# Flamingo-style decoder on one Trainium2 core: the first attention's context values centred by a matmul, its group loop in new orders

## The reference

```python
x = x + tanh(g_xattn[0]) * _L0_xattn_ref(_layernorm(x), ctx, ctx, ...)   # then seven more blocks
# inside, with q = layernorm(x), k = v = ctx, per head:
fg_matrix = cs[:, :, :, None] - cs[:, :, None, :]      # cs: running sum of log sigmoid(forget gate)
log_D = where(causal, fg_matrix, -inf) + igate         # i and f gates: [q, k, v] @ kernel + bias
max_log_D = max(log_D, axis=-1);  D = exp(log_D - max_log_D)
C = (q @ k.T / sqrt(dh)) * D
normalizer = maximum(abs(sum(C, axis=-1)), exp(-max_log_D))
h = (C / (normalizer + 1e-6)) @ v
mean = mean(h);  var = var(h)                          # over the 32 features of a head
out = (h - mean) * rsqrt(var + 1e-6) * outnorm_scale
```

## Time and profile before

| What | Value |
|---|---|
| median of 3 runs | 2186.36 us (2183.57 to 2186.93) |
| the profiled execution, its own time | 2186.99 us |
| its span | 2185.2 us, 41654 instructions |
| busy over the span | PE 88%, VectorE 73%, ScalarE 37%, GpSimd 30% |
| first attention | from 0 to about 149 us |
| in 42.1 to 149.0 us | PE 58.6, VectorE 74.3, ScalarE 50.3, GpSimd 58.5 us busy |

### The profile page before, as it was taken

How to read it: one execution, slowest core, us unless ns; L and a number is a source line. 1 busy time by engine, 2 the same in 40 slices (tenths; PEclk the granted TensorE clock), 3 DMA queues, 4 the chain that set the end, 5 groups by cost and what they waited for, 6 DMA issues and landing times. The chain is left out here.

```text
span 2185.2 us, 41654 instructions
## 1 busy us (share of the span) xinstructions
PE 1930.7 (88%) x14275; PEld 1025.3 (47%) x14275; DVE 1592.2 (73%) x3255; ACT 811.0 (37%) x1491; POOL 662.1 (30%) x903
## 2 busy tenths in 40 slices
PE   4659998998998978999999998979997999979965
PEld 2644444444444434555555554435663444436631
DVE  4768868878878866777777775757884666658978
ACT  4632112012012105555565553315652222226645
POOL 4551102102102104555555553445730000022301
PEclk8559999999999989999999999989997999999966
DMA  4402222222222231000000000000002533311001
GB/s 112 147 18 60 54 45 59 52 45 59 52 45 59 54 83 65 2 2 1 0 0 0 0 2 1 1 6 16 15 6 63 138 79 105 85 38 19 15 1 39
DMA packets 60079, 89.66 MB, mean 41 GB/s; under 512 B 23720, under 2 KB 42024, under 8 KB 55472
## 3 DMA queue, kind: packets, MB, share of 16 engines
q1 hardware_dynamic: 59952, 88.04, 16.4%
HBM read 80.85 MB, written 2.97 MB: 38 GB/s over the span
## 5 line engine op out<-in xcount | busy, mean ns | idle before, releaser
L1021 PE MATMUL l0f_acc<-l0f_z,w_all 128*128 128x512 f32 x512 | 228.8, 609 | 15.0 <-DVE l0f_z L1229 15.0
L916 POOL TENSOR_TENSOR l0f_v<-l0f_val,l0f_top 64x256 f32<-64x256 f32 x128 | 78.2, 611 | 488.1 <-DVE l0f_val L1191 479.5
L970 PE MATMUL l0f_work<-w_all,l0f_xs 128*128 128x512 f32 x384 | 183.5, 600 | 15.2 <-DVE l0f_val L1186 14.5
L1021 PEld LDWEIGHTS l0f_acc<-l0f_z,w_all 128*128 128x128 f32 x512 | 99.1, 195 | 144.1 <-issue 124.2
L241 POOL TENSOR_SCALAR var_eps<-mean_var 128x4 f32<-128x4 f32 (+1 forms) x64 | 14.6, 227 | 474.3 <-DVE mean_var L225 472.2
L1415 PE MATMUL l1x_proj_v<-l1x_wvo,l1x_cs 128*64 128x512 f32 x512 | 134.9, 605 | 0.1
L1191 DVE COPY_PREDICATED l0f_val<-l0f_oh,l0f_work 128x512 f32<-128x512 int32 x160 | 116.6, 729 | 23.7 <-PE l0f_work L970 7.5
L2826 DVE TENSOR_TENSOR l2f_hu<-l2f_act_g,l2f_pu 128x512 f32<-128x512 f32 x104 | 71.1, 684 | 68.8 <-ACT l2f_act_g L2752 67.4
L2752 ACT ACTIVATE l2f_act_g<-l2f_pg 128x512 f32<-128x512 f32 x104 | 61.5, 594 | 149.8 <-PE l2f_pu L2693 138.0
L2701 PE MATMUL l2f_acc<-l2f_hid,w_all 128*128 128x512 f32 x208 | 107.6, 599 | 10.3 <-DVE l2f_hid L2832 10.3
L1641 DVE TENSOR_TENSOR l1x_nm_q<-l1x_proj_q,l1x_rs_q 128x512 f32<-128x512 f32 x64 | 44.2, 691 | 90.3 <-POOL l1x_rs_q L1351 90.3
(11 more groups left out here) (389 smaller groups left out, 4413.1 us busy)
## 6 DMA issues: line engine op xcount, KB each, us to landing
l0f_first_mask<-onehots SPq DMA_DIRECT2D x32, 512.0 KB, 5.7
w_all<-onehots SPq DMA_DIRECT2D x32, 512.0 KB, 11.8
w_all<-combination SPq DMA_DIRECT2D x40, 256.0 KB, 5.3
w_all<-in_weights SPq DMA_DIRECT2D x1, 4640.0 KB, 16.7
l0x_m_b<-running_max SPq DMA_DIRECT2D x16, 256.0 KB, 4.6
w_all<-combination SPq DMA_DIRECT2D x16, 224.0 KB, 4.5
w_all<-combination SPq DMA_DIRECT2D x16, 192.0 KB, 4.2
w_all<-combination SPq DMA_DIRECT2D x16, 160.0 KB, 4.3
```

Of the source, the lines that this page charges most:

```text
L916: nc.gpsimd.tensor_tensor(v2[a * SEQ:(a + 1) * SEQ, t % 2, b, :, :], val[r, t % 2, :, :].rearrange("p (c a) k -> p c a k", a=2)[:, :, a, : ...
L970: nc.tensor.matmul(value_banks[e % 3][:, :], xs[:, t * P:(t + 1) * P], ve[:, e, :], start=True, stop=True).then_inc(ve_done, 1)
L1021: nc.tensor.matmul(acc[:, :], oe[:, n % E, n // E, :], z[:, n % Z, :], start=(n == 0), stop=(n == C * E - 1)).then_inc(acc_done, 1)
```

## The change

GpSimd's context means and its per-group subtraction go. TensorE centres instead: per group, four fp32 matmuls multiply the transposed context by a constant 128 x 128 matrix (identity minus 1/32 within each head), into the PSUM bank `turn`, and ScalarE copies the result into va (`copy_values`). va, hs and den get two buffers. The loops of VectorE and GpSimd are written in another order. The matrix adds 128 columns to the constants.

```diff
-        half_sum = [sb(f"half_sum{i}", [P, TILES // PARTS * NH, DH >> (i + 1)]) for i in range(4)]
-        ctx_mean = sb("ctx_mean", [P, TILES * NH])
...
-        va = sb("va", [P, N, E])
-        hs = sb("hs", [P, N, E])
-        den = sb("den", [P, 3, N])
+        va = sb("va", [P, 2, N, E])
+        hs = sb("hs", [P, 2, N, E])
+        den = sb("den", [P, 2, 3, N])
...
-                def context_means(i):
-                    pool.wait_ge(core.ctx_loaded[i], 16)
-                    w = TILES // PARTS
-                    src = core.ctx_tok[:, i * w:(i + 1) * w, :].rearrange("p j (h e) -> p (j h) e", h=NH)
-                    n = DH
-                    for k in range(5):
-                        n //= 2
-                        dst = half_sum[k][:, :, :] if k < 4 else \
-                            ctx_mean[:, i * w * NH:(i + 1) * w * NH].unsqueeze(2)
-                        nc.gpsimd.tensor_tensor(dst, src[:, :, 0:n], src[:, :, n:2 * n], ALU.add).then_inc(summed, 1)
-                        pool.wait_ge(summed, count(5 * i + k + 1))
-                        src = dst
...
-                    context_means(i)
-                nc.gpsimd.tensor_scalar(ctx_mean[:, :], ctx_mean[:, :], 1.0 / DH, None, ALU.mult).then_inc(mean_ready, 1)
...
-                pool.wait_ge(mean_ready, count(1))
-                pool.wait_ge(ones_set, count(2))
-
-                def centre_values(g):
-                    after(pool, pv_done, g)
-                    means = ctx_mean[:, g * N:(g + 1) * N].rearrange("p (t h) -> p h t", h=NH)
-                    nc.gpsimd.tensor_tensor(va[:, :, 0:DH].rearrange("p (h t) e -> p h t e", h=NH),
-                                            core.ctx_tok[:, g * G:(g + 1) * G, :].rearrange("p t (h e) -> p h t e", h=NH),
-                                            bcast(means, 3, DH), ALU.subtract).then_inc(va_ready, 1)
-
                 def inverse_deviation(g):
                     pool.wait_ge(var_ready, count(g + 1))
+                    after(pool, rs_ready, g)
...
                 for i in range(GROUPS + 5):
-                    if 0 <= i - 4 < GROUPS:
-                        apply_gate(i - 4)
+                    if 0 <= i - 5 < GROUPS:
+                        norm_gpsimd(core, nc, pool, ns, i - 5)
+                    if 0 <= i - 2 < GROUPS:
+                        inverse_deviation(i - 2)
                     if 0 <= i - 3 < GROUPS:
-                        inverse_deviation(i - 3)
-                    if 0 <= i - 1 < GROUPS:
-                        centre_values(i - 1)
-                    if 0 <= i - 4 < GROUPS:
-                        norm_gpsimd(core, nc, pool, ns, i - 4)
+                        apply_gate(i - 3)
...
+                def centre_values(g):
+                    after(pe, va_ready, g)
+                    pe.wait_ge(read, count(4 if g > 2 else 2))
+                    for t in range(G):
+                        ins = nc.tensor.matmul(turn[:, t * P:(t + 1) * P], core.ctxT[:, (g * G + t) * P:(g * G + t + 1) * P],
+                                               core.const("centre"), start=True, stop=True)
+                    ins.then_inc(centred, 1)
...
+                        pe.wait_ge(ones_set, count(2))
...
-                            ins = nc.tensor.matmul(po[r, at:at + E], cmat[r, n, :], va[r, n, :], start=True, stop=True)
+                            ins = nc.tensor.matmul(po[r, at:at + E], cmat[r, n, :], va[r, g % 2, n, :], start=True, stop=True)
...
                 for i in range(GROUPS + 5):
                     if 0 <= i - 1 < GROUPS:
+                        centre_values(i - 1)
                         scores(i - 1)
                     if i == 3:
+                        pe.wait_ge(va_ready, count(3))
                         turn_gates(1)
...
+                def copy_values(g):
+                    act.wait_ge(centred, count(g + 1))
+                    act.wait_ge(ones_set, count(2))
+                    after(act, pv_done, g - 1)
+                    nc.scalar.activation(va[:, g % 2, :, 0:DH].rearrange("p (h t) e -> p t h e", h=NH),
+                                         turn[:, :].rearrange("p (t h e) -> p t h e", t=G, h=NH), ACT.Copy)\
+                        .then_inc(va_ready, 1)
+
                 def copy_sums(g):
                     act.wait_ge(pv_done, count(g + 1))
-                    after(act, scaled_ready, g)
-                    nc.scalar.activation(hs[:, :, :].rearrange("p (i n) e -> p i (n e)", i=2),
+                    after(act, scaled_ready, g - 1)
+                    nc.scalar.activation(hs[:, g % 2, :, :].rearrange("p (i n) e -> p i (n e)", i=2),
                                          po[:, :].rearrange("p (i n) -> p i n", i=2)[:, :, 0:8 * E], ACT.Copy)\
                         .then_inc(hs_ready, 1)
...
                 for i in range(GROUPS + 6):
+                    if 0 <= i - 1 < GROUPS:
+                        copy_values(i - 1)
                     if 0 <= i - 2 < GROUPS:
                         copy_sums(i - 2)
...
-                    after(dve, factor_ready, g)
-                    nc.vector.reciprocal(den[:, 2, :], den[:, 1, :]).then_inc(inv_done, 1)
+                    after(dve, factor_ready, g - 1)
+                    nc.vector.reciprocal(den[:, g % 2, 2, :], den[:, g % 2, 1, :]).then_inc(inv_done, 1)
...
                 for i in range(GROUPS + 6):
-                    if 0 <= i - 3 < GROUPS:
-                        variances(i - 3)
-                    if 0 <= i - 5 < GROUPS:
-                        norm_apply(core, nc, dve, ns, i - 5)
-                    if 0 <= i - 4 < GROUPS:
-                        add_to_x(i - 4)
                     if i == 2:
                         running_max(1)
                         ch.done()
                     if i < GROUPS:
                         exponents(i)
+                    if 0 <= i - 2 < GROUPS:
+                        denominators(i - 2)
+                        square_sums(i - 2)
+                        variances(i - 2)
                     if 0 <= i - 3 < GROUPS:
                         scale(i - 3)
                     if 0 <= i - 1 < GROUPS:
                         decayed_scores(i - 1)
-                    if 0 <= i - 2 < GROUPS:
-                        denominators(i - 2)
-                        square_sums(i - 2)
+                    if 0 <= i - 5 < GROUPS:
+                        norm_apply(core, nc, dve, ns, i - 5)
+                    if 0 <= i - 4 < GROUPS:
+                        add_to_x(i - 4)
...
+    put("centre", np.eye(P) - (p[:, None] // 32 == p[None, :] // 32) / 32.0)
...
```

21 lines of the change are left out of this document (10 added, 11 removed).

## The result

| | before | changed |
|---|---|---|
| median of six runs each | 2186.64 us (2183.57 to 2188.03) | 2196.38 us (2192.86 to 2202.17) |
| the profiled execution, its own time | 2186.99 us | 2202.17 us |
| end of the first attention in it | 148.78 us | 161.76 us |
| from there to the end of the span | 2036.4 us | 2038.6 us |

The account below looks back on a forecast made before the run. The first attention was taken as a ring of waits with no engine full, VectorE's list setting the period. Loop +15.0, first denominators +1.6, tail +2.5 and opening -4.1 summed to +15.0 us on 2186.99: 2202 us, range 2187 to 2212.

Parts of the forecast that it names:

- the ring: Group loop: one turn becomes strictly serial, 10.5 us between products 1 to 4 and 12.8 for 4 to 7; +15.0 us.
- the two copies: Group loop: two ScalarE copies of some 512 columns, one after the other, 0.65 us each, 1.3 per turn.
- The 1.6 for the denominators: Group loop: denominators and variance, plus some 0.1 us to the next instruction, take 1.6 us of each turn.
- the late turns: Group loop from the fifth turn: xn behind the product and four transposes ahead of the values make turns 12.8 us.
- The first denominators: Before product 1: the first seven instructions on den and var now stand ahead of it; +1.6 us.
- Centring: TensorE in the group loop: four new matmuls per group, between 1.94 and 3.88 us, taken as 1.94.
- The fourth rival: Group loop: centring takes 3.88 us, adding 1.94 in six turns, +11.6 us, 2213.6 us; chance 0.06.
- The opening: Before the group loop: GpSimd's halving additions go, gaining between 1.9 and 6.4 us; the middle taken, -4.1 us.
- The tail: After product 7: four normalisations remain instead of three; bounds 0 and +4.8 us, middle taken, +2.5 us.
- The clock's rise (first): Group loop: TensorE's longer bursts raise its clock, its links halve and exponentials decide; +3.4 us, 2190.4 us; chance 0.15.
- The third: Group loop: VectorE's list stays the bound, relieved of GpSimd, period 8.8 us; faster kernel, 2180.9 us; chance 0.06.
- The second: From the opening on: the clock stays up, the feed-forward block starts warm; -2.2 us, 2184.8 us; chance 0.05.

Follow-up runs that it names:

- e7: Changed kernel with ScalarE copying and squaring the sums of group i-2 before copying the centred values of group i-1; 2196.72 us in one profiled execution.
- e2: Changed kernel with denominators, square sums and variances put behind the product on VectorE instead of ahead of it; 2200.42 us in one profiled execution.
- e1: Changed kernel with VectorE's normalisation xn first in the turn again, not behind the product; median 2193.78 us, ratio 1.0030 against before.
- e5: Changed kernel with the four centring matmuls of each group issued twice, writing the same result; 2206.93 us in one profiled execution.
- e9: Changed kernel with GpSimd's halving additions (context means) put back into the opening, result unused; 2208.44 us in one profiled execution.
- e6: e4's kernel with all eight groups centred in the opening and eight buffers for va; median 2172.57 us, ratio 0.9941 against before.
- e4: Changed kernel with VectorE's and GpSimd's loops back in their old orders, GpSimd without its subtraction; median 2182.35 us, ratio 0.9974 against before.

## Why the prediction was right, point by point

**The direction and the ring: right, to 0.2 us a turn.** 10.5 and 12.8 were forecast, 10.54 and 12.65 measured, and products 1 to 7 lie 69.6 us apart for a forecast of 69.9. The parts agree too: the two handovers of TensorE are 1.27 and 3.56 in both, scaling 0.63 for 0.61. Two parts were off and nearly cancelled: centring with its handover is 2.11 instead of 1.94 + 0.05, and the two copies 1.13 instead of 1.3, since the second starts 0.50 after the first (81.02, 81.52), less than its duration of 0.60. The 1.6 for the denominators holds too (1.64), but it rests on a choice of row that the prediction doesn't speak of. It read group 0, where nothing ran beside them; in five of the eight groups of before the first instruction took 1.13 beside GpSimd's gate multiplication, as here one turn ahead of the earlier trace rows:

```profile
86.34 1.13 DVE L739 SCALAR_TENSOR_TENSOR l0x_den<-l0x_hs 128x16 f32<-128x16 f32 x1
```

In the changed kernel it takes 0.18 to 0.19 in all eight groups, as GpSimd waits for the variances then. With 1.13 the sum would have been 11.5. That the ring is what was said is shown by e7 and e2, each of which opens it at one link and brings the early turns to 9.5, and e1 shows the late turns' 2.1 us to be xn's place.

**The first denominators: right.** +1.45 for +1.6. The interval is 11.9 to 12.6 us in the six kernels with the denominators ahead of the product and 10.4 to 10.9 in the four with them behind it, so the sign is sure and the size is not.

**Centring: a mis-sized term, by little.** Eight records of the four matmuls took 2.07 us, with 128 columns, for the lower bound of 1.94 that I took from 64. The weight loads are 1.78 in both cases (for the 64 columns in the earlier trace rows), so the reason for choosing the lower end holds. The fourth rival (3.88) is out. e5 shows that what is added to the centring is added to the turn (1.71 us in the turn from product 1, 1.28 in that from product 4).

**The opening: mis-sized.** -4.1 was the middle of -1.9 and -6.4; -6.2 came. The step that failed is taking the middle: |f| came 5.1 us earlier (32.72 for 37.84), so most of VectorE's delay was passed on, and another 1.0 was gained between |f| and product 0, where the prediction had the chain "shift as it is". e9 ties 5.8 to 6.3 us to the means, so their worth is near the upper bound (6.4). The changed kernel's profile gave back about 1 of it, most likely to the dip of the clock in its opening, and won the 1.3 in the second memory trip. That it came to nearly the upper bound in sum is these two cancelling. TensorE is now busy 5.00 of 5.00 us from 20 to 30, so a further gain in VectorE's normalisation would probably be worth little; no run tries it.

**The tail: about right.** +3.05 for +2.5, within 0 and 4.8.

**The sum.** +14.64 + 1.45 + 3.05 - 6.16 = +13.0 for +15.0; the 2 us between are the opening. The forecast of 2202 is met by the profiled execution's 2202.17 partly by chance: 2.2 of its +15.2 are from the unchanged rest. The median, 2196.4, is 5.6 lower: 2.0 of it the terms explain. The other 3.6 lie between this execution, the slowest of the six, and its fellows, of which there is no trace; whether their attention also ends 13.0 us later is not shown. One sum in the prediction is off: with opening and tail at their bounds its terms give +10.2 and +19.5, which is 2197.2 to 2206.5, not 2196 to 2209.

**The rivals.** The clock's rise (first) did not happen in the changed kernel but does in e5, so its weight was not idle. The third, VectorE's list as the bound, came true only in e6, once both TensorE's chain and the ring were out of the way; its turns, 7.5 to 8.8, are not the 8.8 for all six that the prediction took, as it had the late period of 9.7 stand for the shorter early ones too. The second is out: 0.50 from the first turn on. In e6 the third's effect was measured a second time, 1.11 us for 0.18; the Trainium skill's GPSIMD Engine Reference (Specifications) names contention in SBUF with VectorE instructions that have two inputs there, as this one has, and the trace agrees.

The Trainium skill's TensorE: Matmul & The Clock Gate (What's actually happening) has the low clock as the default, from which activity releases it. In the changed kernel it stayed at 0.50 through every turn, and in e5 it rose with the same pattern and four more 128 x 128 matmuls; the rule holds in direction, and no run here says what it asks for.

## What to carry to other kernels

- Where engines hand work round in a ring, write down the chain from one product to the next with its handovers before judging an order: a step that stands ahead of the shared operation joins the ring, and one behind it lies beside it. A sum from rows was right to 0.2 us a turn, while busy shares said nothing.
- A change made of several edits can hold a gain and a greater loss: undo the orders alone. Here, in the profiles, they cost 20 us on top of a gain of 7.
- Work that needs only loaded inputs is best put into a stretch where its engine waits anyway; ask then which engine's list is full.

## What the runs showed of the hardware

- The clock rose within a burst of TensorE when the 128 x 128 matmuls in it were doubled (0.63 and 0.71 in the two windows above), but not in bursts of small matmuls that kept the engine busy 5.00 of 5.00 us, nor with single centring. In e5 it fell back in the wait behind the burst. Nor was it a matter of busy time alone: in e4 TensorE was busy 4.66 to 5.00 us of every 5 from 85 to 120 us, and the clock stayed at 0.50. What separates these cases I cannot say from these runs.
- A small VectorE instruction that met a 512-column GpSimd operation took 0.33 to 1.20 us instead of 0.16 to 0.18, whichever of the small instructions it was. In each case that was looked at it ended 0.02 to 0.05 us behind GpSimd's operation: the factor of the earlier trace rows at 103.93 (GpSimd at 103.90), the denominators in e6 at 87.55 (87.51), the shortest one, in before, at 77.88 (77.83). So the price was what was left of GpSimd's operation, and it depends on when the two meet. In e4, without GpSimd's subtraction, the factor took 0.17 to 0.18 in all eight groups, for 1.03 to 1.05 in six of before's.
- With the same opening the first product stood anywhere from 49.66 to 51.15 us, the last of these with the clock dip named above, and the unchanged part behind the attention took 2033.4 to 2040.4 us. The store of the running maximum was followed by its loads after 3.60 us in before and after 2.02 in the others. A single execution can't tell differences of a few us here; the stage's own times can.
